# Wide attention in steps of two chunks: maxima seeded into the score banks, the low part of the queries in row tiles

## The reference, cut to what matters

```python
q = (layernorm(x) @ w_q).reshape(B, 256, 16, 64)          # 16 heads of 64
k, v = split(context @ w_kv)                              # 4096 keys and values per batch and head
attn = softmax(einsum('bqhd,bkhd->bhqk', q * 0.125, k))
out = einsum('bhqk,bkhd->bqhd', attn, v).reshape(B, 256, 1024)
```

## Time and profile before

| | us |
|---|---|
| profiled execution, its own time | 4754.62 |
| its span, first to last instruction | 4752.7 |
| the three timed runs, median | 4752.34 |
| PE busy over the span | 4166.2 (88%) |
| DVE, ACT, POOL busy | 2741.3, 2186.9, 1537.8 |
| first scores of wide attention to its last output | 193.28 to 2393.80 |

### The profile page before, as it was taken

The page is one execution under the profiler, slowest core; times in us unless marked ns, Lnnn a source line. Parts: engine busy times, 40 slices in busy tenths (PEclk is TensorE's granted clock), DMA queues, the critical chain, the costliest instruction groups (busy, mean ns, idle before and its releaser), DMA issues. The chain is left out here.

```text
span 4752.7 us, 77711 instructions
## 1 busy us (share of the span) xinstructions
PE 4166.2 (88%) x26758; PEld 2832.8 (60%) x26758; DVE 2741.3 (58%) x4163; ACT 2186.9 (46%) x3893; POOL 1537.8 (32%) x1213
## 2 busy tenths in 40 slices
PE   3799999999999999999977895899999999766499
PEld 1576766666766666766644794555555555333265
DVE  4566555555655556555536412566666677465566
ACT  2455655555555555555524211355555566333111
POOL 2355655555655555565502202200000000023000
PEclk8899999999999999999988897899999999877699
DMA  5744444444444434334220384744444322100011
GB/s 194 247 153 157 148 167 161 160 142 157 157 161 158 170 138 164 128 139 142 86 74 8 131 321 146 228 141 147 134 136 151 115 69 61 29 1 1 13 38 42
DMA packets 217082, 607.29 MB, mean 128 GB/s; under 512 B 43277, under 2 KB 128525, under 8 KB 162445
## 3 DMA queue, kind: packets, MB, share of 16 engines
q1 hardware_dynamic: 214048, 594.34, 37.2%
q0 software_dynamic: 2688, 8.39, 0.5%
HBM read 508.26 MB, written 94.37 MB: 127 GB/s over the span
## 5 line engine op out<-in xcount | busy, mean ns | idle before, releaser
L792 POOL TENSOR_TENSOR wa_acc<-wa_acc,wa_probs 128x512 f32<-128x512 f32 x930 | 1214.7, 1306 | 559.3 <-ACT wa_probs L623 507.1
L677 DVE TENSOR_REDUCE wa_mx<-wa_ps_m 128x2 f32<-128x1024 f32 x512 | 626.6, 1224 | 571.7 <-PE wa_ps_m L494 568.2
L623 ACT ACTIVATE wa_probs<-wa_ps_s 128x512 f32<-128x512 f32 x1024 | 557.5, 595 | 604.2 <-PE wa_ps_s L437 549.8
L1316 DVE TENSOR_REDUCE na_mx<-na_ps_m 128x1 f32<-128x512 f32 x1024 | 639.2, 682 | 207.0 <-PE na_ps_m L1153 207.0
L1264 ACT ACTIVATE na_probs<-na_ps_s 128x512 f32<-128x512 f32 x1024 | 549.8, 600 | 402.7 <-PE na_ps_s L1168 397.3
L436 PE MATMUL wa_ps_s<-wa_qh,wa_keys 128*128 128x256 f32 x2048 | 564.0, 307 | 39.1 <-ACT wa_probs L623 35.8
L448 PE MATMUL wa_ps_o<-wa_probs,wa_values 128*64 128x256 f32 x4096 | 557.4, 393 | 0.0
L437 PE MATMUL wa_ps_s<-wa_ql,wa_keys_one 128*128 128x256 f32 x2048 | 517.7, 285 | 0.0
L436 PEld LDWEIGHTS wa_ps_s<-wa_qh,wa_keys 128*128 128x128 f32 x2048 | 394.1, 192 | 163.3 <-issue 84.7
L462 PE MATMUL wa_ps_k<-wa_ctx,wa_w_k 128*128 128x512 f32 x1536 | 414.2, 406 | 49.3 <-DMA wa_ctx<-ctx_split 49.3
L1153 PE MATMUL na_ps_m<-na_keys,na_q 98*128 98x512 f32 x1024 | 419.1, 417 | 28.4 <-DVE na_mx L1316 17.4
(11 more groups left out here) (334 smaller groups left out, 5108.6 us busy)
## 6 DMA issues: line engine op xcount, KB each, us to landing
wa_ctx<-ctx_split SPq DMA_DIRECT2D x256, 1024.0 KB, 4.9
na_ctx<-ctx_split SPq DMA_DIRECT2D x56, 1024.0 KB, 6.6
na_keys<-k_rows SPq DMA_DIRECT2D x192, 256.0 KB
ctx_split<-wa_stage SPq DMA_DIRECT2D x32, 1024.0 KB, 3.9
wa_land<-in_ctxT SPq DMA_DIRECT2D x32, 512.0 KB, 6.4
ge_w_b<-in_w_rows SPq DMA_DIRECT2D x8, 2048.0 KB
k_rows<-na_k_high SPq DMA_DIRECT2D x64, 256.0 KB, 2.4
k_rows<-na_k_low SPq DMA_DIRECT2D x64, 256.0 KB, 2.2
```

Of the source, the lines that this page charges most:

```text
L623: act.activation(probs[:, c % R, :], ps_s[c % 2][:, :], ACT.Exp).then_inc(exp_done, 1)
L677: dve.tensor_reduce(mx[:, half, :, k], ps_m[:, :, :], AX.X, ALU.max).then_inc(m_taken, 1)
L792: pool.tensor_tensor(acc[:, :], acc[:, :], probs[:, c % R, :], ALU.add).then_inc(summed, 1)
L1316: dve.tensor_reduce(mx[:, j, u:u + 1], ps_m[n % RM][:, :], AX.X, ALU.max).then_inc(m_taken, 1)
```

## The change

- A unit is worked in 16 steps of two chunks. In a step PE does one `maximum`, then `scores` of two chunks: first four matmuls of 64 rows and 256 columns (the high keys by ql, head 0 on rows 0 to 63, head 1 on rows 64 to 127, without a copy with ones), then four of 128 rows (keys by qh). In odd steps two `weigh` stand before and `project_keys` stands after.
- The maxima are no longer two rows of ql. `finish_maximum` writes the negated maxima 128 wide (m_neg), PE turns them by the identity into ps_v, ACT copies the 128x512 to m_wide, and before each use of a score bank ACT writes m_wide into it (`initial`, two per step, 128x512 each); the scores accumulate on top (start=False). There are three score banks, each one head of two chunks; ps_v has one bank in place of two. keys_one and its copies are gone.
- keys are held for two units (keys[i][h]). DVE `take_keys` now copies head 1's high part from ps_k, and then takes both low parts; ACT copies head 0's only.
- Values are projected over both units of a quad (V_STEPS), one half-block in each of 16 of 32 steps, from their own stream v_ctx (two slots); the keys have k_ctx (two slots). Together 12 MB a unit are streamed in place of 8. At the start PE reads the split blocks straight from stage.
- The denominator goes into the other half of ps_o; copy_out and the reciprocal follow it. The last unit is summed by POOL alone. All engines are unrolled, semaphores start at 0, and no memset stands before the first load.

```diff
-        def schedule(fori, start, body, end):
-            with fori(1, 12) as j:
-                body(j, 0)
-                body(j, 1)
 ...
+        V_STEPS = [20 + 2 * n for n in range(12)] + [43, 44, 45, 46]
+        def key_block(t):
+            n = CG + (t + 3) // 2
+            return n if t % 2 and n < G * CG else None
+        def max_unit(t):
+            n = t + 1
+            return (1 + n // ST, n % ST // 2, n % 2) if 1 + n // ST < G else None
 ...
# PE
+            def turn_maximum(g):
+                pe.wait_ge(neg_ready, g + 1)
+                pe.wait_ge(v_ready, 2 * CG + sum(value_unit(t) is not None for t in range(ST * g - 1)))
+                for h in range(2):
+                    for half in range(2):
+                        col = h * SQ + half * P
+                        ins = pe.matmul(ps_v[:, col:col + P], m_neg[:, 2 * half + h, :], ident[:, :], start=True, stop=True)
+                ins.then_inc(mT_done, 1)
+            def scores(t):
+                a, c = t // ST, t % ST * 2
+                n = 2 * t
 ...
+                pe.wait_ge(init_done, n + 2)
+                for i in range(2):
+                    for h in range(2):
+                        r = slice(h * DH, (h + 1) * DH)
+                        pe.matmul(ps_s[(n + h) % BANKS][:, i * SQ:(i + 1) * SQ], keys[a % 2][h][r, (c + i) * P:(c + i + 1) * P],
+                                  ql[a % 3][r, :], start=False, stop=False, skip_group_check=True)
+                for h in range(2):
+                    for i in range(2):
+                        ins = pe.matmul(ps_s[(n + h) % BANKS][:, i * SQ:(i + 1) * SQ], keys[a % 2][h][:, (c + i) * P:(c + i + 1) * P],
+                                        qh[a % 3][:, h, :], start=False, stop=True, skip_group_check=True)
+                    ins.then_inc(s_ready, 1)
 ...
+            for t in range(-3, LAST + 2):
+                a, st = t // ST, t % ST
+                if st == ST - 1 and a + 1 < G:
+                    turn_maximum(a + 1)
+                if t % 2 and t >= 3:
+                    weigh(t - 3)
+                    weigh(t - 2)
+                if st == 1 and t > 1:
+                    denominator(a - 1)
+                unit = max_unit(t)
+                if t >= -1 and unit is not None:
+                    maximum(*unit)
+                if 0 <= t < LAST:
+                    scores(t)
+                kb = key_block(t)
+                if kb is not None:
+                    project_keys(kb)
+                unit = value_unit(t)
+                if unit is not None:
+                    project_values(*unit, turns=(t + 1) // ST + 1)
# ACT
+            def initial(n):
+                act.wait_ge(wide_ready, n // CH + 1)
+                if n >= BANKS:
+                    act.wait_ge(exp_done, n - BANKS + 1)
+                of_head = m_wide[:, n % 2 * SQ:(n % 2 + 1) * SQ].unsqueeze(1).to_broadcast([P, 2, SQ])
+                act.activation(ps_s[n % BANKS][:, :].rearrange("p (c n) -> p c n", c=2), of_head, ACT.Copy).then_inc(init_done, 1)
 ...
+            for t in range(-2, LAST):
+                kb = key_block(t - 1)
+                if kb is not None:
+                    take_keys(kb)
+                if st == ST - 1 and a + 1 < G:
+                    take_maximum(a + 1)
+                    initial((t + 1) * 2)
 ...
+                if t >= 0:
+                    exponents(2 * t)
+                    exponents(2 * t + 1)
+                    initial(2 * t + 3)
+                    if st != ST - 2:
+                        initial(2 * t + 4)
# DVE
+            def take_keys(kb):
+                dve.wait_ge(kproj_done, kb + 1)
 ...
+                dve.tensor_copy(keys[g % 2][1][DH:P, cols], ps_k[DH:P, :]).then_inc(kd_ready, 1)
+                dve.wait_ge(ka_ready, kb + 1)
+                dve.tensor_tensor(keys[g % 2][0][DH:P, cols], ps_k[0:DH, :], keys[g % 2][0][0:DH, cols].bitcast(F32),
+                                  ALU.subtract).then_inc(kl_ready, 1)
+                dve.wait_ge(kd_ready, kb + 1)
+                dve.tensor_tensor(keys[g % 2][1][0:DH, cols], ps_k[DH:P, :], keys[g % 2][1][DH:P, cols].bitcast(F32),
+                                  ALU.subtract).then_inc(kl_ready, 1)
 ...
+            for t in range(-2, LAST + 2):
+                    take_keys(kb)
+                    take_values(*unit)
+                if st == 1 and t > 1:
+                    copy_out(a - 1)
+                    take_maximum(*unit)
+                if st == 1 and t > 1:
+                    divide(a - 1)
+                if st == ST - 2 and 0 <= a < G - 1:
+                    finish_maximum(a + 1)
+                if st == 4 and 0 <= a < BLOCKS - CG:
+                    split_low(a + CG)
```

More of the change, by code:

```diff
@@ L271, in wide_attention @@
         w_high, w_low = s.sem("w_high"), s.sem("w_low")
[L272 to L275, removed]
+        w_stored = [s.sem(f"w_stored{i}") for i in range(2)]
+        opened = s.sem("opened")
+        kproj_done, ka_ready, kd_ready, kl_ready = (s.sem(n) for n in ("kproj_done", "ka_ready", "kd_ready", "kl_ready"))
@@ L312, in value_weights @@
                 for h in range(2):
+                    pair = (2 * q + h) % PAIRS
+                    weights_stored(pair)
                     sp.dma_start(w_v[:, :, :, h * P:(h + 1) * P].rearrange("p a k n -> p (a k) n").bitcast(F32),
[L314 to L321, removed]
-                for half in range(2):
[L323 to L359, removed]
-                    arrived(0, k, k // 2 + 1)
-                    if k >= SLOTS:
-                        sp.wait_ge(vproj_done, 1 + 2 * (k - SLOTS) + 2)
-                    stream(0, k)
-                    if k == 3:
-                        weights_stored(1)
-                        weights(1, 1, 1)
@@ L426, in _ @@
             leave(G - 1)
-            sp.wait_ge(o_stored, 1 + 16 * G)
+            sp.wait_ge(o_stored, 16 * G)
         @block.tensor
         def _(pe):
-            def scores(a, slot, c):
-                pe.wait_ge(exp_done, a * CH + c)
-                cols = slice(c * P, (c + 1) * P)
-                for h in range(2):
-                    out = ps_s[c % 2][:, h * SQ:(h + 1) * SQ]
-                    pe.matmul(out, keys[h][:, cols], qh[slot][:, h, :], start=True, stop=False)
-                    ins = pe.matmul(out, keys_one[h][:, cols], ql[slot][:, h, :], start=False, stop=True)
-                ins.then_inc(s_ready, 1)
@@ L505, in turn_maximum, with weigh @@
                 ins.then_inc(mT_done, 1)
+            def weigh(u):
+                a, hb = u // ST, u % ST
+                pe.wait_ge(exp_done, 2 * u + 2)
+                pe.wait_ge(v_ready, 2 * CG * (a // 2) + hb + 1)
+                if hb == 0 and a:
+                    pe.wait_ge(o_copied, a)
+                for c in (2 * hb, 2 * hb + 1):
+                    for h in range(2):
+                        col = a % 2 * P + h * DH
+                        ins = pe.matmul(ps_o[h * DH:(h + 1) * DH, 0:SQ], values[:, c, col:col + DH],
+                                        probs[:, c % R, h * SQ:(h + 1) * SQ], start=(c == 0), stop=(c == CH - 1))
+                ins.then_inc(pv_done, 1)
@@ L655, in _, with split @@
-            schedule(act.Fori, start, body, lambda: None)
+            def split(n):
+                act.wait_ge(land_in[n % 2], 16 * (n // 2 + 1))
+                if n >= 2:
+                    act.wait_ge(stored[n % 2], 16 * (n // 2))
+                if 2 <= n < CG + 2:
+                    act.wait_ge(kproj_done, n - 1)
+                    act.wait_ge(vproj_done, 2 * (n - 1))
+                act.activation(stage[n % 2][:, 0, :, :], land[n % 2][:, :, :], ACT.Copy).then_inc(high_ready, 1)
```

699 lines of the change are left out of this document (300 added, 399 removed).

## The result

The changed kernel takes 4643.7 us (median of 4 runs, 4641.0 to 4645.5), the kernel before 4753.1 beside it: a ratio of 0.977, 95% interval 0.975 to 0.978, so 109 us less. The prediction was 4650. The profiled execution took 4645.5 with a span of 4643.7.

What follows compares the result with a forecast made beforehand. PE was taken to bound wide attention, 46% of the span. Terms summing to -104 us took the profiled 4754.6 to 4650.6, 4648 for timed runs, stated as 4650; the 8-in-10 range was 4570 to 4770.

Steps and rivals of the forecast that it cites:

- Row tiles: Low score matmuls on PE: pairs of 64 rows run together, saving 0.24 a step over 512 steps, -123 us.
- Loops: Engine loops in wide attention: unrolling removes 5.5 us from each of 11 looped quads, -60 us.
- Start: Start of wide attention: earlier first load, no detour by DRAM and shorter work on the first blocks, -32 us.
- Waits that go: Ends of units: PE's waits for the reduction and the split of the maxima disappear, -55 us.
- Around the denominator: Cycles around the denominator and the other unit's first with values: PE's maximum waits for DVE, 2.9 x 16, +46 us.
- Wait at the turn: Before the maxima are turned: PE waits for DVE, 2.9 or 2.0, mean 2.45 over 31 turns, +76 us.
- Clock behind it: After PE's standstill before the maxima are turned: a slower clock costs 1 us a quad, +16 us.
- Last unit: Last unit: the bank cycle sets 2.65, the other step 2.95, and POOL's last sums take longer, +12 us.
- B: Low scores: row tiles don't overlap when both accumulate on seeded banks, +123 us, 4773; chance 5%.
- C: DVE's lows and maxima: DVE is late in every cycle, 200 cycles get 0.5 longer, 4750 us; chance 10%.
- A: Even steps' scores: ACT's seeds, at 1.06 each, set a slower pace, +142 us, 4792; chance 11%.
- D: Turning of the maxima: waits mostly absorbed, no clock lost, and the start gains its 42; -70, 4580 us; chance 12%.

Runs made afterwards that it cites:

- experiment 1: The changed kernel with its four low score matmuls on all 128 rows instead of 64-row tiles: 4708.8 us, ratio 0.990.
- experiment 5: The kernel before the change with the loops of ACT, DVE and POOL written out straight, SP's loops kept: 4700.0 us, ratio 0.988.
- Experiment 6: The changed kernel with turn_maximum placed after the two weighs of its step instead of ahead of them: 4567.6 us, ratio 0.960.
- Experiment 10: The changed kernel with one weigh a step in the last unit alone: 4637.3 us, ratio 0.975.
- experiments 7 to 9: The changed kernel with the next context's splitting one step later: ACT's and DVE's parts 4613.8 us, only DVE's 4614.0, only ACT's 4623.7.
- experiment 3: The changed kernel with the low score matmuls after the high ones instead of before: 4745.2 us, ratio 0.998.
- experiment 4: The changed kernel with an extra ACT copy of 128x512 to a spare tile ahead of each step's first seed: 4731.9 us, ratio 0.995.
- experiment 2: The changed kernel with one weigh in every step in place of two in every odd step: 4572.2 us, ratio 0.961.

## Why the prediction held, and where it was off

The time was right to 6 us, and most of its steps show in the rows. Some errors cancelled.

- **Row tiles** (-123): -134.2, shown by the step of 1.25 and by experiment 1. 8 of the other 11 us are the loops' slow clock: with the loops written out the same groups of the kernel before cost 753.7 for 761.6.
- **Loops** (-60): -57 by experiment 5.
- **Start** (-32): -31.6. The first split came at 80.62, the first keys at 87.59, the first scores at 163.0 for 161.
- **Waits that go** (-55): both names of the earlier trace rows are gone from the ends of units.
- **Around the denominator** (+46): 41.4, of which 4 lie in the first unit alone (one wait of 2.24, three of 0.64). Forecast 0.3, 2.1, 0.5; the rows show 0.2 and 1.6 in one unit of a quad, 0.3 in the other, and 0.15 to 0.2 a cycle later in most.
- **Turn** (+16): 31 x (1.06 - 0.54) = +16. **Wait at the turn** (+76): 66.3 + 4.1 = 70.4; but 3.36 and 1.07 where 2.9 and 2.0 stood. **Clock behind it** (+16): +29, about 1.6 and at times 2.65 a long wait, where 1 a quad was forecast from another wait. Experiment 6.
- **Last unit** (+12): 63.3 for 38.8, +24.5. The bank's cycle was right (2.61 for 2.65), the odd steps' weighs were priced at full clock. Experiment 10.

Three terms are missing from the sum. **The split of the context**, +23.4: it lies in the one cycle that had no slack left, and I had followed DVE through it without its row L649 (experiments 7 to 9). **The values' bank**, +16.1: 29 times a values group waits 0.56 until DVE has emptied the bank, by the trace; no run gave the second bank back. **Tile shapes of the other groups**, some -70: PE's own work fell by 167.7 in the budget; the forecast had 91 of that, the loops' slow clock accounts for 20 more (experiment 5), and the extra clock at the turns works the other way with 13. I had kept the old prices for weighs, values and keys. Two weighs in a row take 1.88, two single ones 2 x 1.01 (-45 in all); values take 1.53 behind the high scores, where most took 1.62 between groups of other shapes (-16); keys ahead of values take 1.39 and not 1.48 (-5); the last 3 are in the scores. I had counted changes of tile shape for the low part alone, and not for the groups whose neighbours the change exchanges as well. For the low part itself the prediction had some 0.2 a step if it stood alone; experiment 3 shows two changes and 0.36.

Costs that I did not have come to 39.5 + 13 + 12 = 65; against them stand the 70, and 10 of the new waits that came out smaller. That the total is right to 6 us is luck in this part.

Of the rivals, B and C are refuted by the 1.25 and by cycles without a wait; A by the seed of 0.606, with experiment 4 showing that a longer chain on ACT does strike, as A has it, through the scores of even steps, only from a later point on. D (waits at the turn absorbed) did not come, but experiment 6 reaches it by moving the turn.

What stays open: the 3 us by which the rest of the program is longer, and why the slow clock behind a wait of 3.36 costs now 1.4 to 1.6 and now 2.65, and nothing at one of 15 turns.

## What to carry to other kernels

When the bound engine gets faster in a step, price the next engine's whole chain in the tightest cycle, with every rare instruction that lands there (here 2.08 of splitting), and spread the bound engine's work evenly over the steps before making its pieces cheaper: one weigh a step cost 32 us of PE and saved 78 of waits. Put an instruction that waits behind work that doesn't depend on it; a standstill of 3.4 us of PE cost 5. On TensorE count every change between tile shapes in the order of issue, before and after. Beside the marked waits, compare the time from the start of one group to the start of the next: 70 us of waiting in experiment 4 stood in no list of PE's waits.

## What the runs showed of the hardware

- A change of tile shape between groups of matmuls costs 0.18 to 0.19 us where 64 rows meet 128, half of it in the group on either side (experiment 3); a run of weighs (128x64 tiles) broken in two costs 0.14 (1.88 against 2.02). Two 64-row matmuls of 256 columns in different row tiles, both adding onto banks that ACT had written, start within the time of one full one: four in 0.33.
- ACT writes 128x512 from SBUF into PSUM in 0.606 (1024 of them), about as long as its exponential from PSUM (0.595); the prediction had bounded it between 0.50 and 1.06.
- Behind a wait of PE of 1.5 before the turn the granted clock stayed at 1.00 (15 times in experiment 6, and once behind 2.24); behind 1.83 it fell in 13 of 15 turns of experiment 2, behind 3.36 in 14 of 15 of the changed kernel, and so it did in most pairs of steps where 1.44 came back in every second step of the last unit.
- The releaser that the trace names for a wait on several semaphores can be one that merely ended last, here by 0.1 us.
